# Hybrid block on one core: another order of score slots and maxima fills, and the routing of later token groups set sooner

## What is computed

```
x = x + attention(norm(x))     # 16 heads of 64, causal; keys are also the values
x = x + mixture(norm(x))       # 16 experts of 64, top 2 of a sigmoid router, plus a shared expert
x = x + state_space(norm(x))   # projection, convolution, gated scan, norm, projections
x = x + mixture(norm(x))       # the same weights again
```

## Time and profile before

| what | value |
|---|---|
| median of 3 runs | 827.27 us (824.65 to 827.36) |
| the profiled execution's own time | 827.14 us |
| its span in the trace | 825.4 us |
| PE busy | 740.8 us (90%), 5448 matmuls |
| DVE, ACT, POOL busy | 462.3, 390.0, 439.0 us |
| attention | up to about 501 us |
| first mixture, state space, second mixture | about 501 to 642, to 703, to the end |

### The profile page before, as it was taken

One profiled execution on the slowest core, in us unless ns is written; L12 is line 12 of the kernel. 1 busy time (PEld: TensorE's weight loads), 2 busy tenths in 40 slices (PEclk: granted clock), 3 DMA queues, 4 the chain that ended last, 5 costly groups with the idle time before them and its releaser, 6 DMA issues. The chain is left out here.

```text
span 825.4 us, 14251 instructions
## 1 busy us (share of the span) xinstructions
PE 740.8 (90%) x5448; PEld 495.9 (60%) x5448; DVE 462.3 (56%) x1232; ACT 390.0 (47%) x483; POOL 439.0 (53%) x316
## 2 busy tenths in 40 slices
PE   2789999999999999999999989988998856679998
PEld 2456555655555565556556547867887522657787
DVE  5765565666556556655755501555455774655343
ACT  2345556555555555555555441355444740255422
POOL 4356775676667658656855680044343553144343
PEclk9699999999999999999999999999999885899999
DMA  2000000000000000000000006132231000033232
GB/s 64 8 1 1 9 1 1 8 1 2 8 1 2 7 2 1 8 2 1 2 1 26 2 1 147 27 120 87 66 104 39 0 1 0 0 106 113 67 106 77
DMA packets 29459, 25.15 MB, mean 30 GB/s; under 512 B 10128, under 2 KB 20944, under 8 KB 29392
## 3 DMA queue, kind: packets, MB, share of 16 engines
q1 hardware_dynamic: 29392, 24.25, 10.1%
HBM read 22.92 MB, written 1.31 MB: 29 GB/s over the span
## 5 line engine op out<-in xcount | busy, mean ns | idle before, releaser
L378 POOL TENSOR_TENSOR all_x<-all_x,at_probs 128x1024 f32<-128x1024 f32 (+3 forms) x128 | 222.9, 1741 | 35.7 <-ACT at_probs L453 21.0
L453 ACT ACTIVATE at_probs<-at_ring 128x1024 f32<-128x1024 f32 x144 | 147.3, 1024 | 113.8 <-PE at_ring L625 107.3
L498 DVE CUSTOM_DVE_ANT_0 at_ring<-at_ring,at_after_query 128x128 f32<-128x128 f32 (+3 forms) x256 | 119.5, 521 | 74.1 <-PE at_ring L590 74.1
L643 PE MATMUL at_out<-at_probs,at_k_nat 128*64 128x512 f32 (+3 forms) x768 | 140.3, 494 | 1.1 <-DVE a_attn_t L521 0.9
L1079 POOL TENSOR_TENSOR m_prod<-m_gate,m_wb 128x512 f32<-128x512 f32 x64 | 81.8, 1283 | 110.6 <-ACT m_gate L936 85.5
L378 POOL TENSOR_TENSOR all_x<-at_probs 128x768 f32<-128x768 f32 (+1 forms) x32 | 66.9, 2091 | 126.5 <-ACT at_probs L453 126.3
L990 DVE TENSOR_TENSOR m_hid<-m_prod,m_u 128x512 f32<-128x512 f32 x64 | 44.0, 687 | 88.7 <-POOL m_prod L1079 84.4
L643 PEld LDWEIGHTS at_out<-at_probs,at_k_nat 128*64 128x64 f32 x768 | 49.2, 136 | 69.9 <-issue 66.0
L494 DVE TENSOR_REDUCE at_half_max<-at_ring 128x2 f32<-128x1024 f32 x64 | 75.5, 1222 | 12.4 <-PE at_ring L590 12.4
L936 ACT ACTIVATE m_gate<-m_g 128x512 f32<-128x512 f32 x72 | 42.9, 599 | 82.2 <-PE m_g L847 81.7
L855 PEld LDWEIGHTS m_acc<-rest_wd,m_hid 128*128 128x128 f32 x576 | 75.9, 194 | 6.2
(11 more groups left out here) (196 smaller groups left out, 1293.4 us busy)
## 6 DMA issues: line engine op xcount, KB each, us to landing
m_wb<-m_wt_far SPq DMA_DIRECT2D x128, 128.0 KB, 2.9
all_x<-in_L_attn_a_x SPq DMA_DIRECT2D x8, 256.0 KB, 3.7
at_w_raw<-in_L_attn_a_W_qk SPq DMA_DIRECT2D x8, 128.0 KB, 2.6
out<-all_x SPq DMA_DIRECT2D x4, 256.0 KB, 2.3
a_room<-in_L_attn_a_W_out SPq DMA_DIRECT2D x1, 512.0 KB, 4.0
m_raw_wg<-in_L_ffn_experts_wg SPq DMA_DIRECT2D x1, 512.0 KB, 4.8
m_raw_wu<-in_L_ffn_experts_wu SPq DMA_DIRECT2D x1, 512.0 KB, 4.2
rest_wd<-in_L_ffn_experts_wd SPq DMA_DIRECT2D x1, 512.0 KB, 4.2
```

The lines of the kernel that those rows point to most:

```text
L378: return pool.tensor_tensor(sums[:, :, a * P:b * P], left, right, ALU.add)
L453: act.activation(probs[:, :, slot * BANK:(slot + 1) * BANK], pair("S", unit, slot)[:, :, :], ACT.Exp, scale=BETA).then_inc(exp_done, 1)
L498: last = dve.tensor_tensor_reduce(out=sums_ps, in0=sums_ps, in1=after_query[:, BANK - w:BANK], scale=1.0, scalar=MASKED, op0=ALU.add, op1= ...
L643: last = pe.matmul(out_ps[rows(l), o:o + (b - a) * P], k_nat[g % 3][:, j, rows(l)], probs[:, l, at:at + (b - a) * P], start=(j == 0), stop ...
```

## The change

Two tables are changed. In `ROUNDS`, fills 2 and 5 now come first in rounds 2 and 3, and in round 4 the slots come ahead of their fills (slot 7, fill 8, slot 8, fill 9). In the mixtures, every piece that prepares groups 2 and 3 is due two steps sooner, `natural` and `route1` one step sooner; `turn_w` and `w_high` have a due time two steps later in the table, which for group 1 makes one step later and for groups 2 and 3 the old one. For group 0 they come two steps later, which on ScalarE sets the copy of the weights (L965) behind the high part of group 1.

```
--- before.py
+++ after.py
@@ -208,8 +208,8 @@
 
 BURSTS = [[(0, 0), (1, 0), (2, 0), (1, 1)], [(3, 0), (2, 1)], [(4, 0)], [(5, 0), (6, 0)], [(7, 0), (8, 0), (8, 1)]]
 NBURST = len(BURSTS)
-ROUNDS = [[("S", 0)], [("S", 1), ("M", 0), ("S", 2), ("M", 1)], [("S", 3), ("M", 2), ("S", 4), ("M", 3), ("M", 4)],
-          [("S", 5), ("M", 5), ("S", 6), ("M", 6), ("M", 7)], [("M", 8), ("S", 7), ("M", 9), ("S", 8)]]
+ROUNDS = [[("S", 0)], [("S", 1), ("M", 0), ("S", 2), ("M", 1)], [("M", 2), ("S", 3), ("S", 4), ("M", 3), ("M", 4)],
+          [("M", 5), ("S", 5), ("S", 6), ("M", 6), ("M", 7)], [("S", 7), ("M", 8), ("S", 8), ("M", 9)]]
 FIRST_OF_HALF = {0: 0, 1: 1}
 BURST_OF = [max(r for r, b in enumerate(BURSTS) if any(s == slot for s, _ in b)) for slot in range(NSLOT)]
 
@@ -703,7 +703,11 @@
 
 
 PREPARE = dict(statistics=-21, root=-17, norm=-16, residual=-15, turn=-14, high=-13,
-               low=-13, logits=-10, sigmoid=-9, natural=-8, route1=-8, route2=-7, route3=-6, turn_w=-5, w_high=-5)
+               low=-13, logits=-10, sigmoid=-9, natural=-8, route1=-8, route2=-7, route3=-6, turn_w=-3, w_high=-3)
+
+
+SOONER = dict.fromkeys(PREPARE, 2) | dict(natural=1, route1=1)
+SHORT = dict(turn_w=1, w_high=1)
 
 FINISH = dict(add_up=0, statistics=2, root=4, norm=4, turn=6, high=7, low=7)
 
@@ -721,7 +725,7 @@
                 found += [(at, piece, n, t) for t, at in enumerate(SOURCE_TILES[n])] if tiles else \
                     [(SOURCE_ADDED[n], piece, n, 0)]
             if piece in PREPARE:
-                at = PREPARE[piece] + STEPS * n
+                at = PREPARE[piece] + STEPS * n - (SOONER[piece] if n > 1 else n * SHORT.get(piece, 0))
                 if piece == "root" and n == 1:
                     at = PREPARE["sigmoid"]
                 found.append((at, piece, n, "prepare"))
```

## The result

The changed kernel takes 830.37 us (median of 20 runs, 827.66 to 832.22) against 828.85 us for the kernel before on the same chips (20 runs). The ratio is 1.0025, 95% interval 1.0014 to 1.0036: slower by 2.1 us (1.2 to 3.0), within the 0.5% that the forecast called no change. The profiled execution took 830.17 us, its span is 828.4 us: 3.0 us more than before. Read at the first matmul of each sublayer, 1.7 us of them lie in the attention (the first mixture starts at 503.06 instead of 501.32), 0.5 and 0.7 in the two mixtures, 0.05 in the state space. The 1.7 us are of these two executions: the first turned maxima (L600) stand at 37.04 instead of 38.01, before any order of a unit can act, and over the 14 profiles of this study that point moves between 36.45 and 38.31.

What follows compares the result with a forecast made beforehand. TensorE's order was taken as the critical path nearly everywhere. Attention +2.4 us and mixtures -1.8 us gave +0.6 on 827.14: 827.7 us, forecast as no change, range 822 to 832 us.

Steps and rivals of the forecast that it cites:

- Rounds 2 and 3: Attention: the wait for the exponential moves to the second of two fills and gets shorter, gaining 0.10 and 0.08 us.
- Round 4 and the scaling: End of an attention unit: the next outputs wait for VectorE's scaling, covered by the projection alone; 0.30 us lost per unit.
- The sum of a unit: Attention: the loss in round 4 less the gains in rounds 2 and 3, +0.12 us per unit, +1.6 over 13.
- The first unit: Attention: it has no outputs or scaling to wait for, so it keeps round 4's gain: -0.5 us.
- Into the last unit: Attention: no projection covers the chain from fill 9 to the outputs there: +1.5 us, less 0.18.
- Before step 0: Start of a mixture: TensorE reaches step 1 earlier; costed at nothing, since step 2 waits for the first hidden tile.
- Group 1's routing: Mixtures, ahead of TensorE's step 5: the 1.79 us wait gets hidden, gaining 1.3 us in the first, 1.1 in the second.
- Group 2: Mixtures, step 12: the wait for weights becomes one of about 2.3 us for a hidden tile; -0.7 and +0.4 us.
- Group 3: Mixtures: both routing parts stand in one lump on VectorE; 0 in the first mixture and +0.7 us in the second.
- routing off the path: Rival, mixtures: VectorE's lumps fit beside the steps and waits of 5.1 and 4.8 us go; 817 or 822 us; chance 0.16.
- The clock alone: Rival, near step 12: waits in three pieces may keep the clock at 2.4 GHz; 825 us; chance 0.10.
- Fill 9 decides: Rival, between the last fill and the next outputs: they wait over 0.3 us per unit for the scaling; 833 us; chance 0.14.

Runs made afterwards that it cites:

- attn_r4: Kernel before with only round 4 of the attention in the new order: 832.44 us, +4.7 us against the kernel before.
- attn_scale: Kernel before with the attention as changed, and VectorE's scaling of the unit before moved ahead of fill 9's maxima: 825.55 us, -2.5 us against before.
- attn_only: Kernel before with all three changed rounds of the attention, mixtures as before: 831.47 us, +3.3 us against before.
- both_split: Kernel before with the attention of attn_scale and the mixtures of mix_split together: 816.28 us, -10.9 us against before.
- both_soon1: As both_split, but groups 2 and 3 prepared one step sooner than before, not two; their turned weights and copy one step later than before: 817.23 us, -10.3 us.
- mix_group1: Kernel before with only the change for groups 0 and 1 of the mixtures; attention and groups 2 and 3 as before: 828.28 us, +0.2 us against before.
- mix_only: Kernel before with the mixtures as changed, attention as before: 828.56 us, +0.7 us against before.
- mix_split: Mixtures as changed, but the second and third routing parts only one step sooner; attention as before: 818.20 us, -9.4 us against before.
- mix_late4: Kernel before with its old tables, only turn_w and w_high due one step later for every group: 819.75 us, -7.7 us against before.
- attn_r23: Kernel before with only rounds 2 and 3 of the attention in the new order: 825.36 us, -3.0 us against before.

## Why the prediction was right, and where it was not

The forecast of no change held, and 830.37 us is in the range, near its upper end. The attention held by its mechanism. In the mixtures it was partly luck: terms that were off by 2 us and more in both directions nearly cancelled. The steps, one by one:

- *Rounds 2 and 3*: right. Predicted gains 0.10 and 0.08, measured 0.11 in both; the wait moved to the second fill and became shorter. The profile shows it inside a group and not as a wait of its own, as the text had said it would be.
- *Round 4 and the scaling*: right in mechanism and size. Predicted +0.30 a unit, measured +0.27 (period 29.03 against 28.76 in `attn_r4`). `attn_scale` shows that it is the scaling that the outputs wait for.
- *The sum of a unit*: +0.12 predicted, +0.04 measured. It is a difference of terms, each right to 0.03 us, and so three times too large.
- *The first unit*, -0.5: from the first L600 to the third it is 55.01 us in the kernel after and 55.87 in `attn_only`, and 56.1 to 56.7 in the six profiles with the old attention; as far as profiles that differ so much can tell, it is right or somewhat too small.
- *Into the last unit*: +1.3 predicted, and this unit is longer by 1.6 (28.8 instead of 27.2). What the term left out was the clock: a stretch at 1.2 GHz behind the wait of 1.75 to 1.89 us in 2 of 6 profiles, 1.6 and 1.7 us each time (36.60 against 34.97 us from L600 to the first mixture, and 36.26 in `both_split` against 34.54 in `both_soon1`). The attention came to +3.3 instead of +2.4. The mean granted clock of the six runs of `attn_only` is 0.952, of the kernel before beside them 0.954; that is an estimated 4 us more at half clock, which costs 2. That the clock makes up the rest is likely from this, not measured by itself.
- *Before step 0, "this I cost at nothing"*: wrong. The argument went by the hidden tile, and in the first mixture the second product of step 2 does come as before to 0.6 us. But TensorE, earlier at its wait, gathers its idle time in one piece or nearly so, and the low clock that was hidden ahead of step 2 falls behind it: 1.39 us in `mix_group1`. From that product to step 3 it is 1.5 to 2.0 us in 9 of the 10 mixtures with the old tables, and 3.0 to 3.9 in all 18 with new ones (with the turn of group 2 in it, some 0.3, where that comes two steps sooner). Step 3 is 1.2 us later in the kernel after and 2.0 in `mix_group1`, 0.6 of which are weights that came later from DRAM.
- *Group 1's routing, -2.4*: the wait went, as said, and in `mix_group1` steps 3 to 9 of both mixtures take 1.1 and 1.2 us less, against 1.3 and 1.1 predicted. But the kernel gained nothing (+0.2), since the step above took it back. In the kernel after these steps take 2.5 and 2.4 us less; about 0.3 of that has only moved, as the turn of group 2 now stands ahead of step 3.
- *Group 2, -0.7 and +0.4*: the mechanism was right, the wait changed its name at the predicted step. The size was not: +1.5 and +2.8 us from step 9 to 15 (22.4 and 22.5 us instead of 20.9 and 19.6). The lump is 6.04 us long where 5.2 were reckoned, since the first routing part cost 2.16 and not 1.45 (570.19 to 572.35; its 4-element sum alone 0.84, beside GpSimd's residual), the wait 3.33 and not 2.3, and the low clock behind it lasts longer than the old one. In `mix_only`, where that stretch did not come, it is 19.8 us in the first mixture.
- *Group 3, 0 and +0.7*: from step 15 to 24, +0.2 and 0.0. "2.45 us and more" was misread for this group: the kernel before waited only 0.86 us for its weights there, and 0.85 in the second mixture.
- *The sum*: the terms of the second mixture, -1.1, +0.4 and +0.7, make 0.0 and not the +0.2 of the text, so the mixtures should have stood at -2.0 and the forecast at 827.5 us, no change as well.

The mixtures came to +0.7 (-0.2 to +1.7) rather than -1.8. **The step that failed is the price of a wait**: I reckoned waits by their length alone, and named the clock only in a rival, and there as a gain; and at step 12 the length itself was 1.0 us too short.

Of the rivals, *routing off the path* did not come with this change, but its price was real: the 5 to 10 us are what `mix_split` and `mix_late4` win. Against it stood the second routing part on the wrong side of a hidden tile. *The clock alone* had the right mechanism and the wrong sign: the clock did decide a part, but one long wait of 3.33 us was left at step 12. *Fill 9 decides* named a chain that is real, 0.37 us a unit between L600 and the outputs, over the 0.3 that it had set as its sign. Its price did not come, since rounds 2 and 3 win their share (`attn_r23`).

The Trainium skill (SBUF — State Buffer, Who interferes with whom) says that a VectorE instruction with two SBUF inputs contends with a GpSimd instruction that reads SBUF, and that the ports they share are an exclusive lock. The rows agree: 0.84 and 1.10 us for 4 and 8 elements, both ending within 0.03 us of a GpSimd instruction. Of what the prediction drew from the rule, the lump 1.1 us shorter did not come; what came was its last clause, GpSimd's residual falling into the lump.

## What to carry to other kernels

Between two deadlines of the bounding engine, add up everything that another engine does in one stretch; splitting such a lump with the deadline's own operation (here a hidden tile) turned tables that won nothing (+0.7) into ones that win 9.4 us. It is not the only way: giving TensorE's transposes one step more of room in the old order won 7.7, while removing a wait ahead of the one that decides (`mix_group1`) won nothing. Price a wait of TensorE by what the clock does behind it too: gathering short waits into a long one cost 1.39 us here, more than the 1.2 that the removed wait saved. And a unit that lacks the work that covers a chain (here the projection, in one unit of 16) wants an order of its own.

## What the runs showed that I had not expected

- The same wait, in the same code, is followed by a stretch at 1.2 GHz in one execution and not in another: 1.75 to 1.89 us in the attention in 2 of 6, 3.3 us in 5 of 6. Others were alike in all: waits for the weights of 2.2 to 2.5 us in 13 of 13, of 4.6 to 5.4 us at step 2 in 9 of 9, those of 1.5 to 1.8 us for the weights of group 1 in 0 of 8. One profile of each kernel can therefore not tell a difference of 2 us in a mixture: with unchanged tables the first mixture took 141.7, 143.9, 142.8, 141.9 and 142.7 us.
- ScalarE's copy of group 0's weights stands 32.8 us behind the start of the first mixture in all 14 profiles, but from there to GpSimd's first product with them it took 5.8 to 7.3 us (535.85 to 541.68 in the kernel after, 535.10 to 542.04 in `mix_group1`), and in the second mixture 5.7 to 8.2.
